# A cross-attention layer stack: openings of L0 in a new order with tokens through DRAM, products of the first two batches ahead of the others at each norm, and pj in unbroken turn

## The reference, cut to what matters

```
# L0: cross-attention with grouped keys, 32 heads of 16, 8 key/value heads, then a norm
q = x @ Wq + bq;  k = ctx @ Wk + bk;  v = ctx @ Wv + bv
x = norm(x + softmax(q k^T / 4 + mask) v @ Wo + bo)
# L1: two pre-norm cross-attentions (16 heads of 128, one extra bias key and value each) ...
for i in (1, 2):
    h = layernorm_i(x)
    x = x + softmax((h wq_i + bq_i) [ctx wk_i + bk_i; bias_k_i]^T / sqrt(128)) [ctx wv_i + bv_i; bias_v_i] @ wo_i + bo_i
# ... and an MLP of width 2048
x = x + gelu(layernorm(x) @ w_fc1 + b_fc1) @ w_fc2 + b_fc2
```

## Time and profile before

| | |
|---|---|
| time, median of three runs | 2500.95 us (2495.45 to 2508.18) |
| profiled execution: its time, its span | 2500.87 us, 2499.0 us |
| mean granted TensorE clock | 0.974 |
| busy PE, DVE, ACT, POOL | 2319.4 us (93%), 1397.6 (56%), 996.5 (40%), 786.4 (31%) |
| DMA | 248.60 MB, mean 99 GB/s |

### The profile page before, as it was taken

One profiled execution on the slowest core, in us unless ns is written; L12 is line 12 of the kernel. 1 busy time (PEld: TensorE's weight loads), 2 busy tenths in 40 slices (PEclk: granted clock), 3 DMA queues, 4 the chain that ended last, 5 costly groups with the idle time before them and its releaser, 6 DMA issues. The chain is left out here.

```text
span 2499.0 us, 36057 instructions
## 1 busy us (share of the span) xinstructions
PE 2319.4 (93%) x13176; PEld 2074.8 (83%) x13176; DVE 1397.6 (56%) x3138; ACT 996.5 (40%) x2191; POOL 786.4 (31%) x847
## 2 busy tenths in 40 slices
PE   6698899999999999998988979999999999999988
PEld 5576789998989999997776758898999899998976
DVE  4697544454565455456538965454545654455564
ACT  3596433242433333243128953243434333242420
POOL 4132322415141422414541332415141422415055
PEclk8899999999999999999998999999999999999999
DMA  8341223233323323234363213223332323233222
GB/s 254 100 133 44 85 86 110 81 89 119 97 83 95 94 86 110 81 89 138 118 191 101 76 39 101 85 85 119 94 96 86 94 86 110 81 91 117 81 71 80
DMA packets 136996, 248.60 MB, mean 99 GB/s; under 512 B 35663, under 2 KB 57295, under 8 KB 135799
## 3 DMA queue, kind: packets, MB, share of 16 engines
q1 hardware_dynamic: 93327, 123.54, 16.7%
q10 hardware_dynamic: 43496, 122.76, 16.0%
HBM read 221.35 MB, written 27.65 MB: 100 GB/s over the span
## 5 line engine op out<-in xcount | busy, mean ns | idle before, releaser
L622 POOL TENSOR_SCALAR wk_hi<-raw 128x512 fp32r<-128x512 f32 (+1 forms) x84 | 53.6, 638 | 905.4 <-DMA raw<-in_wk 751.1
L1325 ACT ACTIVATE probs<-scores,prm 112x376 f32<-112x376 f32 x256 | 147.0, 575 | 342.5 <-DVE prm L1682 342.4
L755 PE MATMUL pj_two<-ctx_hi,wk_hi 128*128 128x376 f32 x736 | 253.0, 344 | 10.6 <-POOL wk_lo L624 4.6
L756 PE MATMUL pj_two<-ctx_lo,wk_hi 128*128 128x376 f32 x736 | 248.3, 337 | 0.0
L757 PE MATMUL pj_two<-ctx_hi,wk_lo 128*128 128x376 f32 x736 | 247.6, 336 | 0.0
L1466 DVE TENSOR_TENSOR rr<-pj_two,rr 128x448 fp32r<-128x448 f32 (+2 forms) x200 | 132.8, 665 | 163.2 <-ACT rr L1102 163.1
L624 POOL TENSOR_TENSOR wb_lo<-raw,wb_hi 128x512 fp32r<-128x512 f32 x152 | 200.4, 1318 | 12.7
L1468 DVE SCALAR_TENSOR_TENSOR k_lo<-pj_two,cur,k_hi 128x375 fp32r<-128x375 f32 x172 | 104.4, 607 | 169.7 <-ACT k_hi L1104 169.7
L1104 ACT ACTIVATE k_hi<-pj_two,cur 128x375 fp32r<-128x375 f32 x172 | 98.6, 573 | 247.6 <-PE pj_two L757 242.7
L760 PE MATMUL tp_two<-ident,probs 112*126 112x112 f32 (+1 forms) x1152 | 163.8, 267 | 33.8 <-ACT probs L1245 18.2
L760 PEld LDWEIGHTS tp_two<-ident,probs 112*126 112x126 f32 (+1 forms) x1152 | 146.2, 160 | 56.3 <-ACT probs L1245 18.8
(11 more groups left out here) (246 smaller groups left out, 6640.1 us busy)
## 6 DMA issues: line engine op xcount, KB each, us to landing
nat<-nat_scratch ACTq DMA_DIRECT2D x256, 384.0 KB, 3.7
raw<-in_wq SPq DMA_DIRECT2D x72, 256.0 KB, 3.2
raw<-in_wo SPq DMA_DIRECT2D x72, 256.0 KB, 2.6
raw<-in_wk SPq DMA_DIRECT2D x64, 256.0 KB, 3.8
raw<-in_wv SPq DMA_DIRECT2D x64, 256.0 KB, 4.1
raw<-in_w SPq DMA_DIRECT2D x64, 256.0 KB, 2.9
nat_scratch<-rr ACTq DMA_DIRECT2D x7, 1536.0 KB, 6.8
qo<-queries_scratch SPq DMA_DIRECT2D x128, 56.0 KB, 2.4
```

Source lines behind the costliest of these rows:

```text
L622: nc.gpsimd.tensor_scalar(hi, src, 1.0, 0.0, ALU.mult, ALU.add).then_inc(split_hi, 1)
L755: nc.tensor.matmul(dst, l_hi, r_hi, start=first, stop=False)
L756: nc.tensor.matmul(dst, l_hi, r_lo, start=False, stop=False)
L1325: nc.scalar.activation(probs[0:L, h, 0:SK], scores[n % SCR][0:L, 0:SK], ACT.Exp, bias=neg_max[0:L, h:h + 1], accum_out=row_sum[0:L, h:h + ...
```

## The change

In half 0's opening the order is new, and `c` and `x` in it mean that ACT and DVE split a context batch or the tokens there. Tokens are copied from DRAM to DRAM (`x_copy`), loaded from there with two transfers into `pt_hi` and `pt_lo` (not into `raw`), and split by ACT (high) and DVE (low) in two pieces. POOL makes only the high part of L0's key weights and DVE the low part (`wk0_rest`). The memset of `qo` stands at the program's start in half 0. The SP queue is reordered: in half 0 the stores of queries 1 to 3 stand between the others, quarter 0's queries come with four transfers of 448 columns, and half 1's tokens are loaded and split, and its key weights' low part made, during half 0's MLP. Half 1's opening has a new order too.

At each of the three norms of a half, the query (or first MLP layer) products of batches 0 and 1 (224 columns) go ahead of the transposes of batches 2 and 3, in four banks of their own (`q_banks`: those of the scores and of `tp`), and those of the other 224 columns follow the norm. In half 0's MLP the context transposes stand between the heads. The ring `pj` has no padding: a unit's bank is its running number modulo 3.

```diff
+def pre_order(half):
     if half == 0:
-        order = "n0 n1 k0 k1 n2 n3 q0 k2 vt0 k3 vt1 v0 q1 vt2 v1 q2 vt3 v2 q3 v3"
+        order = "c0 n0 c1 k0 n1 k1 c2 n2 vt0 x0 k2 q0 vt1 v0 c3 n3 q1 vt2 v1 k3 q2 vt3 v2 q3 v3"
     else:
-        order = "k0 q0 k1 vt0 q1 vt1 v0 k2 q2 vt2 v1 k3 q3 vt3 v2 v3"
...
+def first_order(a, g):
     left = normed_first(a, g)
     keys = [("k", 0, h) for h in range(HPG)]
     x = [("x", b) for b in left]
+    qa = [("qa", h) for h in range(HPG)]
     if len(x) == HB:
-        return x[0:1] + keys[0:2] + x[1:2] + keys[2:4] + x[2:4]
+        return x[0:1] + keys[0:2] + x[1:2] + keys[2:4] + qa[0:1] + x[2:3] + qa[1:3] + x[3:4] + qa[3:]
     if len(x) == 2:
...
-MLP_PAD = [padded(n) - n for n in MLP_U]
...
+MLP_HEADS = [[("q", 0), ("q", 1), ("n", 0), ("q", 2), ("n", 1), ("q", 3), ("n", 2)], [("q", h) for h in range(HPG)]]
+MLP_MID = [len(names) for names in MLP_HEADS]
+MU = [places(names + [("o", b) for b in range(HB)]) for names in MLP_HEADS]
...
+    x_dram = nc.dram_tensor("x_copy", (D, B * L), F32, kind="Internal").ap()
...
+        x_came = [p[:].rearrange("p h n -> p (h n)")[:, 0:2 * T].rearrange("p (c n) -> p c n", c=2).bitcast(F32) for p in (pt_hi, pt_lo)]
...
+        q_banks = scores + tp
...
-                        sp.wait_ge(rows_empty, hf + 1)
-                    cols = slice(b * L, (b + 1) * L)
+                        if b == 0:
+                            sp.wait_ge(q0_out[c], (hf + 1) * 32)
+                        cols, landed = slice(b * L, (b + 1) * L), q0_in[b]
                     for kv in range(KV2):
                         for r in range(2):
                             at = 64 * kv + 32 * r
                             sp.dma_start(qo[at:at + 32, 4 * kv:4 * kv + 4, cols].bitcast(F32),
                                          q_dram[hf, c, 4 * kv:4 * kv + 4, :, :, cols].rearrange("j e d t -> (e d) j t")
-                                         ).then_inc(q0_in[b], 16)
+                                         ).then_inc(landed, 16)
+                def load_x(half):
+                    sp.wait_ge(x_copied, half * 16 + 16)
+                    for i in range(2):
+                        sp.dma_start(x_came[i], x_dram[2 * i * P:2 * (i + 1) * P, half * T:(half + 1) * T].rearrange(
+                            "(c p) n -> p c n", p=P)).then_inc(x_t_in, 16)
+                def copy_x(half):
+                    cols = slice(half * T, (half + 1) * T)
+                    sp.dma_start(x_dram[:, cols], x_t[:, cols]).then_inc(x_copied, 16)
...
+                if hf == 0:
+                    copy_x(0)
                 load_q0(base + RAW_Q0, 0)
-                for c in range(DC - 1):
-                    load_x(c)
+                load_v0(0)
+                if hf == 0:
+                    load_x(0)
+                load_v0(1)
                 if hf == 0:
                     store_keys0(0, *pre_split("k", 0))
-                load_x(DC - 1)
-                if hf == 0:
                     sp.dma_start(rows8_dram[0], bias_v).then_inc(rows8_in, 16)
                     sp.dma_start(rows8_dram[1], bv).then_inc(rows8_in, 16)
                     store_keys0(1, *pre_split("k", 1))
+                    load_q0(base + RAW_Q, 1)
+                    load_keys0(0, 0)
+                    load_keys0(0, 1)
+                    sp.wait_ge(pj_free, pre_freed("n", 2, SC - 1) + PJ)
+                    load_mask()
+                    load_q0(base + RAW_Q + 1, 2)
+                    store_keys0(2, *pre_split("k", 2))
+                    store_queries0(0, *pre_split("q", 0))
+                    load_q0(base + RAW_Q + 2, 3)
+                    load_queries0(0, 0)
+                    load_keys0(0, 2)
+                    sp.wait_ge(rows8_in, 32)
+                    for i in range(2):
+                        sp.dma_start(rows8[i], rows8_dram[i]).then_inc(rows8_in, 16)
...
+                    store_queries0(1, *pre_split("q", 1))
+                    store_keys0(3, *pre_split("k", 3))
+                    store_queries0(2, *pre_split("q", 2))
+                    load_keys0(0, 3)
+                    store_queries0(3, *pre_split("q", 3))
...
+                            copy_x(1)
...
                         sp.dma_start(came[1][b], ctx_dram[:, b, :].rearrange("(c p) n -> p c n", p=P)).then_inc(ctx_in[b], 16)
+                    sp.wait_ge(pj_ready, gpj + unit["r", HB - 1, DC - 1] + 1)
+                    sp.wait_ge(ex_in, 16 + NG * HB * 48)
+                    sp.sem_inc(sp_passed, 1)
...
+            empty_rows()
             def split_free(n, shape, hi, lo, signal, k, done, keep=False, scaled=None):
                 slot = n % 2
...
-            def keys0(n, use, scaled):
+            def keys0(n):
                 for i in range(2):
-                    src = raw[:, i, :].rearrange("p (x k e d) -> p x k e d", k=KV2, e=2, d=HD0)[:, :, :, 0, :]
-                    hi, lo = (f[:, 2 * P * i:2 * P * (i + 1)].rearrange("p (x k d) -> p x k d", k=KV2, d=HD0) for f in wk0_parts)
+                    src, hi, _ = wk0_pieces(i)
                     pool.wait_ge(raw_ready[i], raw_landed(n + i))
-                    nc.gpsimd.tensor_scalar(src, src, SCALE0, 0.0, ALU.mult, ALU.add).then_inc(raw_scaled, 1)
-                    pool.wait_ge(raw_scaled, scaled + i + 1)
-                    nc.gpsimd.tensor_scalar(hi, src, 1.0, 0.0, ALU.mult, ALU.add).then_inc(split_hi, 1)
-                    pool.wait_ge(split_hi, n + i + 1)
-                    nc.gpsimd.tensor_tensor(lo, src, hi.bitcast(F32), ALU.subtract).then_inc(w_ready["k"], 2)
-                    pool.wait_ge(w_ready["k"], use * DC + 2 * (i + 1))
-                    pool.sem_inc(raw_free[i], 1)
+                    nc.gpsimd.tensor_scalar(hi, src, SCALE0, 0.0, ALU.mult, ALU.add).then_inc(split_hi, 1)
...
+            def q_head(h, slot, use, dst, cols):
+                for c in range(DC):
+                    if h == 0:
+                        pe.wait_ge(w_ready[slot], use * DC + c + 1)
+                    last = three(dst[:, cols], [w[slot][:, c, h * P:(h + 1) * P] for w in (w_hi, w_lo)],
...
+            def q_unit(unit, h, slot, use):
+                pe.wait_ge(pj_free, unit + 1)
+                q_head(h, slot, use, pj[unit % PJ], slice(0, T)).then_inc(pj_ready, 1)
+            def q_first(h, slot, use):
+                q_head(h, slot, use, q_banks[h], slice(0, L2))
+            def q_second(h, slot, use):
+                q_head(h, slot, use, q_banks[h], slice(L2, T)).then_inc(pj_ready, 1)
...
-                    last = three(pj[unit % PJ][0:L, :],
+                    last = three(pj[(base + unit) % PJ][0:L, :],
...
+                    for name in first_order(a, g):
                         if name[0] == "k":
                             keys1(0, name[2])
+                        elif name[0] == "qa":
+                            if name[1] == 0:
+                                pe.wait_ge(ln_lo, (hf * NL + a) * 2 * HB + 4)
+                                pe.sem_inc(pe_passed, 1)
+                            q_first(name[1], "b", use_q)
                         else:
                             normed(hf * NL + a, name[1], gpj + gu[name])
                     if g == 0:
                         pe.wait_ge(ln_lo, (hf * NL + a + 1) * 2 * HB)
                         pe.sem_inc(pe_passed, 1)
-                    q_stage(gpj + gu["q", 0], "b", use_q)
+                    for h in range(HPG):
+                        if g == 0:
+                            q_second(h, "b", use_q)
+                        else:
+                            q_unit(gpj + gu["q", h], h, "b", use_q)
                     scores1(0, 0)
                     scores1(0, 1)
...
+                slot, use = w1_use(hf, 0)
+                pe.wait_ge(ln_lo, (hf * NL + ATT) * 2 * HB + 4)
+                pe.sem_inc(pe_passed, 1)
+                q_first(0, slot, use)
                 normed(hf * NL + ATT, 2, at["x"])
-                normed(hf * NL + ATT, 3, at["x"] + 1, pad=2)
+                q_first(1, slot, use)
+                q_first(2, slot, use)
+                normed(hf * NL + ATT, 3, at["x"] + 1)
+                q_first(3, slot, use)
...
+                    slot, use = w1_use(hf, m)
+                    for name in MLP_HEADS[hf]:
+                        if name[0] == "n":
+                            natural_third(1, m, mpj + mu[name], name[1])
+                        elif m == 0:
+                            q_second(name[1], slot, use)
+                        else:
+                            q_unit(mpj + mu[name], name[1], slot, use)
...
+            def split_x(half):
+                act.wait_ge(x_t_in, (half + 1) * 32)
+                for i in range(2):
+                    nc.scalar.activation(h_hi[:, 2 * i:2 * i + 2, :], x_came[i], ACT.Copy).then_inc(tok_hi, 1)
...
+            def wk0_rest(half):
+                for i in range(2):
+                    src, hi, lo = wk0_pieces(i)
```

(14 more changed lines are left out.)

331 lines of the change are left out of this document (170 added, 161 removed).

## The result

The changed kernel takes 2464.25 us (median of four runs, 2460.03 to 2469.45) against 2502.82 us for the kernel before beside it: a ratio of 0.9845, 95% interval 0.9823 to 0.9868. The profiled execution took 2464.88 us with a span of 2463.0.

The account below looks back on a forecast made before the run. TensorE is busy 93% of the span, so gains come from idle time or a low clock. 20 + 16 + 10.4 + 2 + 8.5 + 7 + 2 = 65.9 us off 2500.87 gives 2435 us, range 2412 to 2465.

Parts of the forecast that it names:

- First opening, 20 us: Half 0's start up to tile 8: earlier query stores and copied tokens remove waits, tile 8 at 71; 20 us, range 12 to 29.
- the sum "14.9 + 50.1 = 65.0": First opening: PE's work done without waits from 14.90 would end at 65.0, 25.9 us earlier than 90.90.
- The step on the tokens ("so this lies beside other work"): First opening: the 0.92 MB token copy, load and split take some 10 to 12 us, beside other work.
- Rival 1: First opening bound by transfers: 21.2 MB at 256 GB/s end at 83 us, gaining 8 instead of 20; chance 0.17.
- The signs: First opening: scores below 60 us, last query store before them, no wait above 5 us before tile 8, clock above 0.85.
- Rest of L0, 0 us: L0's attention of half 0 after tile 8: no change forecast, 0 us.
- Second opening, 16 us: Half 1's start up to tile 8: tokens ready beforehand and earlier stores; 16 us, range 11 to 19.
- Norms of L1, 12.4 us: Early products fill PE's waits at L1's norms: 10.4 us for layer 0's two, 2 for layer 1's.
- 2 for the ring: Group boundaries: the first unit no longer waits for the last output's evacuation; 2 us, range 0 to 3.
- MLP of half 0, 4 + 7 us: Half 0's MLP: 4 us from early products at its norm, 7 from transposes between heads in the passes.
- MLP of half 1, 4.5 us: Half 1's MLP norm: waits as long as in layer 0, filled by early products; 4.5 us.
- The slower case (a late token copy): First opening: SP waits for a late token copy, stopping the opening, tile 8 at 149, 2513 us or more; chance 0.04.

Follow-up runs that it names:

- Run 1: Changed kernel storing only an eighth of half 0's transposed context in the first opening; tile 8 at 67.98 us, 2457.45 us in all.
- run 2: Changed kernel with queries 3 stored ahead of batch 3's keys (half 0) and of batch 2's key store (half 1); 2456.4 us.
- run 9: Changed kernel with half 0's loads of query weights 1 and 2 right behind batch 0's key store, weights 3 also earlier; 2470.16 us.
- run 12: run 8 plus run 10's products and half 0's batch 3 key store behind the last query store; 2448.6 us.
- Run 3: Changed kernel with the DRAM copy of half 1's tokens issued later, in L1's first group of half 0; 2459.26 us.
- run 8: Changed kernel with the three moves of run 2, Run 3 and run 4 together; 2453.14 us.
- run 6: As run 5, but the query products are 48 of 448 columns instead of 96 of 224; 2474.8 us.
- run 7: Changed kernel with half 0's MLP heads in a row and the three context transposes behind them; 2476.2 us.
- run 4: Changed kernel with half 1's tokens loaded behind the first four w1 loads of half 0's MLP; 2461.23 us.
- run 11: run 12 plus the early query weights of run 9; 2452.91 us.
- run 5: Changed kernel with the 224-column products of batches 0 and 1 behind the last norm at all six norms; 2481.37 us.
- run 10: Changed kernel with half 0's MLP norm alone having its products behind it, 48 of 448 columns; 2456.76 us.

## Why the prediction was right, and where it wasn't

**Direction and range** held; the size was 38.6 for 66 us, and the two openings and half 0's MLP account for it, with a loss in L0 that was put at nothing.

**First opening, 20 us: mis-sized, 8.4.** The step that failed is the sum "14.9 + 50.1 = 65.0": I took PE's busy us and let all but some 6 us of waits go, as if PE's work were what the stage waits for. Rows 2 already had DMA at 0.80 and 256 GB/s. Run 1 shows that the transfers hold it up: 5.5 MB less brought 14.6 us. The step on the tokens ("so this lies beside other work") held: their copy landed in 6.2 us, and PE waited 0.66 us for them, at 30.43:

```profile
30.43 0.44 PE L794 MATMUL pj_two<-h_hi,wb_hi 128*128 128x448 f32 x1 [0.66 <-DVE h_lo L1656]
```

The stall of 15.76 us did shrink, to 7.43, by the mechanism named, earlier stores. Nor is it the sum of the bytes alone. With the same bytes in another order tile 8 came 2 us earlier (run 2) and 4 later (run 9), and in run 12, with batch 3's 0.77 MB put behind the last query store, nearly 8 us earlier: what counts is which bytes stand ahead of the last query store. Rival 1, which I gave 0.17, had the place to half a microsecond; that close it is luck, as its one rate stands for 283 GB/s first and 188 later, and run 12 beats it by 8 us with 0.8 MB less. The signs say the same: the first scores were to start below 60 (69.47), the last query store ahead of them (75.72), no wait to be above 5 us (5.15 and 7.43); only the clock came nearly as forecast (0.94 and 0.84 in the page's first two slices, for above 0.85).

**Rest of L0, 0 us: 4.2 slower.** I followed half 1's token copy only to where it is used and not to what stands behind it on SP. Run 3 gives all of it back (130.29).

**Second opening, 16 us: mis-sized, 7.3.** Tokens and key weights were ready, as forecast, and the clock rose. Run 2 shows 3.5 us of the rest to be SP's order. PE's wait of 3.66 us for query weights and 0.79 of DMA look like the first opening; bytes were not varied here, so this part is argued only. The sign (at most 40 us) failed even in run 8, with 41.7.

**Norms of L1, 12.4 us, and 2 for the ring: 15.4 together.** Right. The waits of the earlier trace rows at all norms fell from 41.9 to 16.8 us. By stage, run 6 is 11.4 us longer than the changed kernel in these four, which is the placement less the splitting, and the cost per norm was sized right by the rows. What the unbroken ring and the four banks brought was not measured alone.

**MLP of half 0, 4 + 7 us: 4.9.** The interleaved heads are worth 7.3 us in their three stretches and 7.9 in all, by run 7, as forecast; one wait for `qo` stays, in the first pass:

```profile
1167.97 0.58 PE L799 MATMUL pj_two<-ident,ctx_lo 128*125 128x128 f32 x1 [2.57 <-DVE qo L1566]
```

The early products bring nothing at its norm. The tokens' load makes w1 late (about 3 us forecast; the first split came 3.2 us later) and PE stands in order: the transposes of batch 2 wait behind products that wait for w1. I saw this and still wrote 4. But that is only half of the account. With the load behind w1, the stretch takes 32.24 and 34.09 us with early products (runs 4 and 8) and 34.15 and 32.83 without (runs 12 and 11); with the load ahead, 35.1 in the mean of five with them and 33.0 to 34.1 without (runs 5, 6 and 10). So the late w1 costs some 2 us where the products are early, and even without it they bring nothing here, where 4 was forecast. A wait for w1 of 1.97 us (run 4) and 2.26 (run 8) is still there; why the rest is missing stays open. Without early products the stretch is also 2 to 3 us shorter than the 35.99 of before, and no run shows which edit brings that. **MLP of half 1, 4.5 us: 3.6.** Right.

The slower case (a late token copy) did not show; that copy landed in 6.2 us.

## What to carry to other kernels

Before a stage with idle PE time is priced by PE's busy sum, divide its bytes by the rate at which it already moves them. If the time comes out near the stage's own, look for fewer bytes, or for a better choice of which go first, and take the quotient for a warning and not for a bound: here one order of nearly the same bytes beat it by 8 us. A DMA that is added is paid by what stands behind it, on its issuing queue and on the engines, perhaps half a stage away. Work put ahead into a wait must have all its inputs there: where one of them is late, in-order issue turns the gain into a new wait for what follows.

## What the runs showed of the hardware

A load of 256 KB took 12 us from issue to use while 1536 KB stores and others were under way, and had a median of 7.9 us to landing in the first opening, where the whole kernel's median for the same load is 3.3. The issue of four stores of 188 KB took SP 9.31 us there, and 3.86 in run 1 with 5.5 MB of other stores left out. 96 products of 224 columns took 1.0 to 1.1 us more than 48 of 448, in runs 5 and 6 as in the rows.
